# Other slots for the side work of a scan: when four blocks of one core do their parts beside a recurrence

## The chip, the cores and the metric

The kernel runs on one core of a Trainium2 chip. The metric is the device time of one execution in microseconds (us). The median over three runs before the change is 5640.24 us. The engines are named as in the profile: PE (TensorE, matmuls), DVE (VectorE), ACT (ScalarE), POOL (GpSimd) and SP (the queue that issues the DMAs).

## What is computed

A sequence of four blocks on x of 8 batches, 512 steps and 256 columns, each with a residual and a layer norm after it:

```python
x = layernorm(x + L0_attn(x))   # state space scan: z, conv, dt, B, C; state 512 x 128 per batch
x = layernorm(x + L0_ffn(x))    # silu(x w1) * (x w2), then gelu(h1), gelu(h2), w3
x = layernorm(x + L1_attn(x))   # rms norm, q k v, running sums of exp(k) and exp(k)*v, swiglu
x = layernorm(x + L1_ffn(x))    # 8 experts, the best two of each row
# inside L0_attn, step by step:
h = exp(dt * A_mean) * h + dt * B * u ;  y = C . h
y = rms(y) * norm_w * silu(z) ;  out = y @ out_proj
```

The change touches the placing of L0_attn's end (z, the norm of y, its gate, the projection), of the first layer norm, of L0_ffn's gate and up products and of all of L1_attn. The arithmetic of each step stays.

## The kernel before

The program has three phases: `project_phase` (up to 384 us of the span), `stream_phase` (to 4707.6 us, a tail after the last body included) and `expert_phase`. All that is changed lies in `stream_phase`.

The scan there is cut into `CHUNKS` = 8 chunks of 64 steps; the code of a chunk is called a body here, body 0 to body 7. A body has 256 slots. One slot n advances one step t = n // 4 for a pair of batches g = n % 4; two slots are one half step k = n // 2 (128 in a body). Per slot POOL multiplies 384 columns of the state by their decay (`decay_state`, L1548) and DVE adds the outer product that PE has put in a bank (`add`, L1586). Per half step DVE decays the other 128 columns (`keep`, L1576), ACT takes two exponentials for the half step three ahead (`exp_dve`, L1205, from a bank that PE's `e_rows`, L820, fills; `exp_pool`, L1200, whose rows an SP DMA brings), and PE contracts the state with C (`contract`, L832). POOL may run at most four slots ahead of DVE's adds (it waits on `h_ok`), and it needs `exp_pool` of its half step.

Everything else is the mix: the four blocks' work on the chunk before (m = c - 1), and L1_attn of the chunk before that (m - 1). It is put by hand between the steps of the scan. Body 0 has no mix, body 1 has one without L1_attn (`attn` is False), bodies 2 to 7 have all of it. What stands first in each engine's program order runs first:

- PE at slot n: waits for add(n), makes the outer product for slot n + 2, then the mix products whose `_AT` tuple names n, then, at an even n, `e_rows` for half step k + 3; `contract(k)` comes after slot 2k + 1. All mix products share one bank, `M0`; `bank_read` makes each wait until the one before it, in order of slots, has been read.
- ACT at half step k: every 32nd k a copy of y, then `out_of_bank` for slots 2k - 1 and 2k (it copies products out of M0 and takes tanh), then `exp_dve(k + 3)` and `exp_pool(k + 3)`, then `aside(k)`: the norms, squares and roots whose tables name k. A root (L1216 to L1219) loads an activation table, then takes ln and exp.
- DVE at half step k: add(2k), `keep(k + 1)`, mix(2k), add(2k + 1), mix(2k + 1). The mix there holds `silu_z` (L1607), `gate` (L1614, y by rstd by silu z), `add_gated` (L1623) and `statistics` (L1592, L1596), `spread` (L1601, 128 x 4), `silu_gate` (L1628), `hidden` (L1634), `weigh` (L1649), the scans `sum_weights` and `sum_values` (L1657, L1662), `denominator`, `invert`, `divide`.

Chains that cross engines: root_var(1) on ACT, then `spread` on DVE at slot `SPREAD_AT[1]`, then NORM_1, X_SQ, root_x, TO_UNIT on ACT, then the transposes XN on PE, QK, QK_SQ, root_qk, QK_UNIT, the transposes KT and QT, V, and the scans. The other one: Z, silu_z; Y_SQ, root_y; `gate` at `Y_GATE_AT` (the first waits for root_y); GT, O, `add_gated`, root_var(0), NORM_0, XT, then gate and up. Weights come in units of 512 KB into a ring of four slots (`WRING`); their order `FULL` follows `FIRST_USE`, and each is asked for on SP at the half step `DONE_AT` + 3 of the unit four before it.

Of the kernel before, what the change touches and what calls it, by code (L numbers as in the profile page):

```python
# [75 lines left out]
def project_phase(nc, bank, d, used):  # L76
# [3 lines left out]
    with ExitStack() as ctx:  # L80
# [231 lines left out]
        def _(dve):  # L312
# [60 lines left out]
            with dve.Fori(1, BATCH) as s:  # L373
# [52 lines left out]
GATE_AT = (44, 48, 52, 56, 60, 64, 68, 72)
UP_AT = (46, 50, 54, 58, 63, 66, 71, 74)
H1_AT = ((76, 78, 80, 82), (85, 87, 89, 91), (94, 96, 98, 100), (102, 104, 106, 108), (112, 114, 116, 118), (120,
    122, 124, 126), (129, 131, 133, 135), (138, 140, 142, 144))
H2_AT = ((147, 149, 151, 153), (156, 158, 160, 162), (165, 167, 169, 171), (178, 180, 182, 184), (190, 192, 194,  # L430
    196), (204, 206, 208, 210), (214, 216, 218, 220), (224, 226, 228, 230))
SWI_AT = (174, 176, 188, 189)
OUT_AT = (201, 203)
W3_AT = ((234, 235, 236, 237, 238, 239, 240, 241), (242, 243, 244, 245, 246, 247, 248, 249))

USED_AT = {**{("z", i): (n, n) for i, n in enumerate(Z_AT)}, **{("xn", i): (n, n) for i, n in enumerate(XN_AT)},
           **{("qk", i): (n, n) for i, n in enumerate(QK_AT)}, **{("gT", i): (n, n) for i, n in enumerate(GT_AT)},
# [24 lines left out]
TAIL = ("wz", "qk", "wo", "v", "w1a", "w2a", "w1b", "w2b", "swi", "wout", *(f"h1{j}" for j in range(KH)),  # L462
        *(f"h2{j}" for j in range(KH)), "w3a", "w3b")
WRING = 4
SILU_Z_AT = (4, 5, 8, 10)
SILU_GATE_AT = (47, 51, 55, 59, 63, 67, 71, 75)
SILU_SWI_AT = (180, 183)
ROOT_AT = (16, 0, 103)
SPREAD_AT = (35, 3, 210)
ROOT_X_AT = 2  # L470
ROOT_Y_AT = 4
ROOT_QK_AT = 12
Y_GATE_AT = (13, 15, 17, 21)
CW_AT = (80, 87)
CKV_AT = (99, 108)
SEED_AT = 19
KEEP_AT = (54, 68)
DEN_AT = (114, 124)
REC_AT = (121, 131)
DIV_AT = (141, 149)  # L480
STATS_2_AT = (206, 207)
NORM_1_AT = {2: (0, 1, 2, 3)}
X_SQ_AT = {2: (0, 1, 2, 3)}
TO_UNIT_AT = {2: (0,), 3: (1, 2, 3)}
Y_SQ_AT = {0: (0,), 1: (1,), 2: (2, 3)}
QK_SQ_AT = {7: (0,), 8: (1,), 9: (2,), 10: (3,)}
QK_UNIT_AT = {12: ((0, 1), (1, 1)), 13: ((2, 1), (3, 1)), 14: ((0, 0), (1, 0)), 15: ((2, 0), (3, 0))}
NORM_0_AT = {17: (0,), 18: (1, 2, 3)}
NORM_2_AT = {106: (0,), 108: (1, 2, 3)}
LATER = 3  # L490
STORE_AT = (OUT_AT[1] + 16) // 2
# [1832 lines left out]
```

## Time and profile before

| | us |
|---|---|
| median of 3 runs | 5640.24 |
| lowest, highest | 5631.48, 5642.22 |
| profiled execution | 5622.6 |
| its span | 5620.9 |

Slots are located by DVE's adds: each L1586 instruction is one slot, 256 to a body. The first adds of bodies 0 to 7 start at 384.0, 839.4, 1330.2, 1837.2, 2345.9, 2864.7, 3368.3 and 3876.5 us, and the last one at 4379.7. Slot 32 of bodies 1 to 7 starts at 912.0, 1402.6, 1911.1, 2424.1, 2940.0, 3445.2 and 3948.9; slot 80 at 1007.1, 1497.0, 2005.5, 2521.9, 3035.4, 3540.6 and 4043.3. A row of the view by stretch tells for such a window how long each engine was busy; in a stretch where an engine is busy nearly all the time, that engine bounds it.

### The profile page before, as it was taken

What the parts mean: (1) busy time and instruction counts of PE and PEld (TensorE: products, weight loads), DVE (VectorE), ACT (ScalarE), POOL (GpSimd) and SP (SyncE); (2) the same over time, 40 slices, a digit from 0 to 9 for tenths busy, and PEclk for the clock granted to TensorE, in tenths of its full rate; (3) what the DMA queues carried; (4) which work ended last, traced back from release to release, by engine and by line L of the source; (5) the groups of instructions that cost most, each with busy time, mean ns of one, the idle gap of its engine ahead of it and who ended that gap; (6) DMA issues with size and microseconds to landing.
All of it is one profiled execution on the core that took longest, in us unless ns stands there. A gap on an engine that the chain in (4) does not pass through costs nothing. (4 is left out here: it accounts for less than half of the span.)

```text
span 5620.9 us, 68943 instructions
## 1 busy us (share of the span) xinstructions
PE 4751.0 (85%) x20772; PEld 1734.7 (31%) x20772; DVE 3908.9 (70%) x4276; ACT 3396.4 (60%) x3971; POOL 3984.9 (71%) x2256
## 2 busy tenths in 40 slices
PE   5439998998999899998989998998999784399992
PEld 3301112223223222222232232222222343266662
DVE  7848888888988898889889888988998403000003
ACT  4536666778776877777777778777777431111112
POOL 2359998999999899889989998998999100400004
PEclk8755557999999999899999999998999896699996
DMA  2347666777776667766766776776767121233333
GB/s 89 101 155 257 241 240 218 265 255 245 245 259 250 225 250 248 254 227 240 258 235 246 260 262 221 251 266 236 249 248 260 64 75 54 105 107 108 109 111 112
DMA packets 312933, 1138.41 MB, mean 203 GB/s; under 512 B 69664, under 2 KB 123424, under 8 KB 306720
## 3 DMA queue, kind: packets, MB, share of 16 engines
q1 hardware_dynamic: 298688, 1065.24, 53.7%
q0 software_dynamic: 13920, 69.22, 3.6%
q8 instruction: 158, 2.59, 0.2%
q14 instruction: 167, 1.37, 0.1%
HBM read 1077.17 MB, written 69.73 MB: 204 GB/s over the span
## 5 line engine op out<-in xcount | busy, mean ns | idle before, releaser
L1548 POOL TENSOR_TENSOR s_h<-s_decay,s_h 128x768 f32<-128x768 f32 x2048 | 3707.2, 1847 | 288.6 <-ACT s_decay L1200 256.0
L1586 DVE TENSOR_TENSOR s_h<-s_h,bank 128x1024 f32<-128x1024 f32 x2048 | 2470.1, 1215 | 398.3 <-POOL s_h L1548 211.5
L1200 ACT ACTIVATE s_decay<-s_decay,s_a_neg 128x1536 f32<-128x1536 f32 x1024 | 1605.8, 1568 | 117.2 <-DMA s_decay<-dt_rows 116.4
L832 PE MATMUL bank<-s_h,s_cdiag 128*32 128x512 f32 x8192 | 1262.0, 692 | 7.7 <-ACT s_y L1212 6.8
L1205 ACT ACTIVATE bank<-bank,s_a_neg 128x512 f32<-128x512 f32 x1024 | 672.8, 657 | 759.9 <-PE bank L820 757.1
L806 PE MATMUL bank<-s_vrow,s_brow 9*128 9x512 bf16 x4096 | 846.0, 423 | 268.8 <-DVE s_h L1586 241.5
L1576 DVE TENSOR_TENSOR s_h<-bank,s_h 128x512 f32<-128x512 f32 x1024 | 698.8, 682 | 0.6 <-ACT bank L1205 0.5
L806 PEld LDWEIGHTS bank<-s_vrow,s_brow 9*128 9x128 bf16 x4096 | 208.3, 92 | 1498.9 <-issue 1495.5
L944 PE MATMUL bank<-m_mb,m_w 128*128 128x512 f32 x1024 | 521.2, 638 | 0.9 <-ACT m_mb L1278 0.9
L930 PE MATMUL bank<-m_ma,m_w 128*128 128x512 f32 x1024 | 516.3, 633 | 0.0
L820 PE MATMUL bank<-s_drow,s_unit 3*128 3x512 bf16 x1024 | 432.8, 423 | 78.5 <-DMA s_drow<-dt_parts 49.5
L1935 POOL DMA_INDIRECT e_pj<-in_pj,e_rows x23 | 21.6, 939 | 555.0 <-PE bank L1965 554.4
L2066 ACT ACTIVATE e_hid<-bank 128x512 f32<-128x512 f32 x184 | 109.9, 597 | 495.2 <-PE bank L1965 495.2
L1965 PE MATMUL bank<-e_cT,e_fc 128*128 128x512 f32 x736 | 321.8, 595 | 2.0 <-DVE e_cT L2174 2.0
L1965 PE MATMUL bank<-e_pj,e_hid 128*128 128x256 f32 x1472 | 321.4, 379 | 0.0
L2174 DVE COPY e_cT<-bank 128x512 f32<-128x512 f32 x24 | 16.6, 692 | 415.1 <-PE bank L2006 415.1
L832 PEld LDWEIGHTS bank<-s_h,s_cdiag 128*32 128x32 f32 x8192 | 169.8, 114 | 402.5 <-issue 388.4
L1965 PEld LDWEIGHTS bank<-e_pj,e_hid 128*128 128x128 f32 x1472 | 278.0, 190 | 36.9
L820 PEld LDWEIGHTS bank<-s_drow,s_unit 3*128 3x128 bf16 x1024 | 96.4, 94 | 492.1 <-issue 469.0
L944 PEld LDWEIGHTS bank<-m_mb,m_w 128*128 128x128 f32 x1024 | 182.6, 196 | 201.2 <-issue 201.0
L930 PEld LDWEIGHTS bank<-m_ma,m_w 128*128 128x128 f32 x1024 | 181.3, 194 | 200.1 <-issue 200.1
L1925 POOL MEMSET e_eps<- 128x1 f32 x1 | 0.1, 98 | 329.6 <-POOLq L2253 329.6
(197 smaller groups left out, 4098.9 us busy)
## 6 DMA issues: line engine op xcount, KB each, us to landing
s_decay<-dt_rows SPq DMA_DIRECT2D x1024, 768.0 KB, 5.3
m_w<-in_units SPq DMA_DIRECT2D x210, 512.0 KB, 5.1
s_vrow<-v_parts SPq DMA_DIRECT2D x1024, 36.0 KB
s_brow<-b_parts SPq DMA_DIRECT2D x1024, 9.0 KB
v_parts<-p_part SPq DMA_DIRECT2D x24, 512.0 KB, 3.0
slots<-in_x_tiles SPq DMA_DIRECT2D x128, 96.0 KB, 4.7
e_xs<-slots SPq DMA_DIRECT2D x24, 512.0 KB, 9.6
expert_out<-e_made SPq DMA_DIRECT2D x23, 512.0 KB, 9.2
```

What stands on the lines that cost most here:

```text
L806: mm = pe.matmul(bank[:, X0 + n % 2 * PAIR + b], brow[q:q + PAIRS, buf, hf, at * STATE:(at + 1) * STATE], vrow[q:q + PAIRS, buf, hf, at * ...
L820: pe.matmul(bank[:, E0 + hf], unit[q:q + PARTS], drow[q:q + PARTS, buf, t % STEPS], start=True, stop=True).then_inc(e_ps, 1)
L832: mm = pe.matmul(bank[q * 32:(q + 1) * 32, Y0], cdiag[:, hf * LANES + q, at * BLK:(at + 1) * BLK], h[:, t % 2, hf * LANES + q], start=(at ...
L930: mm = pe.matmul(bank[:, j % 4 if tail else M0], w[:, slot, k * P:(k + 1) * P], ma[:, k], start=(k == 0), stop=(k == KH - 1))
L944: mm = pe.matmul(bank[:, j % 4 if tail else M0], w[:, slot, k * P:(k + 1) * P], mb[:, k], start=(k == 0), stop=(k == KH - 1))
L1200: act.activation(decay[:, k % RING], decay[:, k % RING], ACT.Exp, scale=a_neg[:, 1:2]).then_inc(decay_ok, 1)
L1205: act.activation(bank[:, E0 + k % HALVES], bank[:, E0 + k % HALVES], ACT.Exp, scale=a_neg[:, 1:2]).then_inc(e_ok, 1)
L1548: pool.tensor_tensor(h[:, t % 2, g * PAIR:(g + 1) * PAIR, DCOLS:], decay[:, k % RING, g % 2 * PAIR:(g % 2 + 1) * PAIR], h[:, (t + 1) % 2, ...
L1576: dve.tensor_tensor(h[:, t % 2, hf * LANES:(hf + 1) * LANES, 0:DCOLS], bank[:, E0 + hf].rearrange("p (b d) -> p b d", b=LANES), h[:, (t + ...
L1586: dve.tensor_tensor(h[:, t % 2, g * PAIR:(g + 1) * PAIR], h[:, t % 2, g * PAIR:(g + 1) * PAIR], bank[:, X0 + n % 2 * PAIR:X0 + (n % 2 + 1) ...
L1965: mm = pe.matmul(dst, lhs(k), rhs(k), start=(k == 0), stop=(k == n - 1))
L2066: act.activation(hid[:, r, m], bank[:, m % 4], ACT.Gelu).then_inc(up_ok, 1)
```

## The change

Only the tables of slots and half steps change. Of the products, z goes from slots 1, 3, 5, 7 to 0, 2, 4, 6; the transposes of gated y from 21 to 24 to 14, 15, 16, 18; the projection from (27, 28), (30, 31) to (20, 21), (23, 25). L1_attn comes after them: its transposes from 9, 12 to 26, 28, q and k from 14 to 19 to 30 to 36, the transposes of k and q from 32 to 36 to 60, 68 and 64, 70, in between the gate and up products, which begin at 41 for 44, and v from 39, 42 to 73, 74. The norms and squares of half steps 2 and 3 are spread over 4 to 12; root_var(1) goes from half step 0 to 3 and its spread from slot 3 to 7; the gate of y goes from slots 13 to 21 to 10 to 14 while root_y stays at half step 4; root_qk goes from 12 to 21 and the q and k norms from 12 to 15 to 23 to 29. From slot 79 on, scans, reciprocals and a few more move by one to six slots. With the slots the order of the weight units changes: wz, wo, qk, w1a, w2a, w1b, w2b, v for wz, qk, wo, v, w1a, w2a, w1b, w2b.

```diff
--- before.py
+++ after.py
@@ -414,22 +414,22 @@
 X_CREDIT = BUFS * GROUPS * STEPS
 E_CREDIT = BUFS * HALVES * STEPS
 
-Z_AT = (1, 3, 5, 7)
-XN_AT = (9, 12)
-QK_AT = (14, 15, 17, 19)
-GT_AT = (21, 22, 23, 24)
-O_AT = ((27, 28), (30, 31))
-KT_AT = (32, 34)
-QT_AT = (35, 36)
-XT_AT = (40, 43)
-V_AT = (39, 42)
-GATE_AT = (44, 48, 52, 56, 60, 64, 68, 72)
-UP_AT = (46, 50, 54, 58, 63, 66, 71, 74)
-H1_AT = ((76, 78, 80, 82), (85, 87, 89, 91), (94, 96, 98, 100), (102, 104, 106, 108), (112, 114, 116, 118), (120,
+Z_AT = (0, 2, 4, 6)
+XN_AT = (26, 28)
+QK_AT = (30, 31, 34, 36)
+GT_AT = (14, 15, 16, 18)
+O_AT = ((20, 21), (23, 25))
+KT_AT = (60, 68)
+QT_AT = (64, 70)
+XT_AT = (37, 40)
+V_AT = (73, 74)
+GATE_AT = (41, 45, 49, 54, 57, 61, 65, 69)
+UP_AT = (43, 48, 51, 55, 59, 63, 67, 72)
+H1_AT = ((75, 77, 79, 81), (86, 88, 90, 92), (94, 96, 98, 100), (102, 104, 106, 108), (112, 114, 116, 118), (120,
     122, 124, 126), (129, 131, 133, 135), (138, 140, 142, 144))
 H2_AT = ((147, 149, 151, 153), (156, 158, 160, 162), (165, 167, 169, 171), (178, 180, 182, 184), (190, 192, 194,
     196), (204, 206, 208, 210), (214, 216, 218, 220), (224, 226, 228, 230))
-SWI_AT = (174, 176, 188, 189)
+SWI_AT = (174, 176, 187, 188)
 OUT_AT = (201, 203)
 W3_AT = ((234, 235, 236, 237, 238, 239, 240, 241), (242, 243, 244, 245, 246, 247, 248, 249))
 
@@ -462,30 +462,30 @@
 TAIL = ("wz", "qk", "wo", "v", "w1a", "w2a", "w1b", "w2b", "swi", "wout", *(f"h1{j}" for j in range(KH)),
         *(f"h2{j}" for j in range(KH)), "w3a", "w3b")
 WRING = 4
-SILU_Z_AT = (4, 5, 8, 10)
-SILU_GATE_AT = (47, 51, 55, 59, 63, 67, 71, 75)
-SILU_SWI_AT = (180, 183)
-ROOT_AT = (16, 0, 103)
-SPREAD_AT = (35, 3, 210)
-ROOT_X_AT = 2
+SILU_Z_AT = (3, 5, 8, 9)
+SILU_GATE_AT = (44, 48, 52, 56, 60, 64, 68, 72)
+SILU_SWI_AT = (179, 181)
+ROOT_AT = (14, 3, 103)
+SPREAD_AT = (33, 7, 210)
+ROOT_X_AT = 9
 ROOT_Y_AT = 4
-ROOT_QK_AT = 12
-Y_GATE_AT = (13, 15, 17, 21)
-CW_AT = (80, 87)
-CKV_AT = (99, 108)
-SEED_AT = 19
-KEEP_AT = (54, 68)
-DEN_AT = (114, 124)
-REC_AT = (121, 131)
-DIV_AT = (141, 149)
-STATS_2_AT = (206, 207)
-NORM_1_AT = {2: (0, 1, 2, 3)}
-X_SQ_AT = {2: (0, 1, 2, 3)}
-TO_UNIT_AT = {2: (0,), 3: (1, 2, 3)}
-Y_SQ_AT = {0: (0,), 1: (1,), 2: (2, 3)}
-QK_SQ_AT = {7: (0,), 8: (1,), 9: (2,), 10: (3,)}
-QK_UNIT_AT = {12: ((0, 1), (1, 1)), 13: ((2, 1), (3, 1)), 14: ((0, 0), (1, 0)), 15: ((2, 0), (3, 0))}
-NORM_0_AT = {17: (0,), 18: (1, 2, 3)}
+ROOT_QK_AT = 21
+Y_GATE_AT = (10, 11, 13, 14)
+CW_AT = (79, 91)
+CKV_AT = (96, 102)
+SEED_AT = 36
+KEEP_AT = (57, 68)
+DEN_AT = (117, 125)
+REC_AT = (122, 131)
+DIV_AT = (145, 151)
+STATS_2_AT = (205, 206)
+NORM_1_AT = {4: (0,), 5: (1,), 6: (2, 3)}
+X_SQ_AT = {6: (0, 1), 7: (2,), 9: (3,)}
+TO_UNIT_AT = {10: (0,), 11: (1, 2), 12: (3,)}
+Y_SQ_AT = {0: (0,), 2: (1,), 3: (2, 3)}
+QK_SQ_AT = {15: (0,), 16: (1,), 17: (2,), 19: (3,)}
+QK_UNIT_AT = {23: ((0, 1),), 24: ((1, 1), (2, 1)), 25: ((3, 1),), 27: ((0, 0), (1, 0)), 29: ((2, 0), (3, 0))}
+NORM_0_AT = {15: (0,), 16: (1, 2), 17: (3,)}
 NORM_2_AT = {106: (0,), 108: (1, 2, 3)}
 LATER = 3
 STORE_AT = (OUT_AT[1] + 16) // 2
```

## Rows read from the trace of the kernel before

**Rows 1.** by stretch: its bounds, length, busy us (instructions), clock, DMA.

```profile
384.00:839.40 455.40, 436.44 (x1656) 59.75 (x1656) 384.53 (x384) 279.09 (x274) 455.40 (x258) 0.50 0.69 245
839.40:912.00 72.60, 60.80 (x263) 17.48 (x261) 60.15 (x61) 45.65 (x58) 63.23 (x34) 0.71 0.57 211
1330.20:1402.60 72.40, 59.24 (x289) 19.09 (x286) 58.29 (x63) 67.06 (x113) 59.66 (x33) 0.89 0.63 218
1837.20:1911.00 73.80, 60.07 (x288) 19.53 (x285) 57.35 (x62) 67.21 (x113) 58.72 (x33) 0.86 0.58 212
1911.00:2005.50 94.50, 84.37 (x422) 26.26 (x422) 87.86 (x97) 70.24 (x87) 85.36 (x48) 1.00 0.68 236
3876.50:3948.90 72.40, 59.24 (x288) 19.08 (x285) 58.16 (x62) 67.06 (x113) 59.62 (x33) 0.89 0.62 223
```

**Rows 2.** POOL in body 0, in body 3's slots 0-31, 32-79.

```profile
L1548 POOL TENSOR_TENSOR s_h<-s_decay,s_h 128x768 f32<-128x768 f32 x258 | 459.0, 1812 | 0.0
...
L1548 POOL TENSOR_TENSOR s_h<-s_decay,s_h 128x768 f32<-128x768 f32 x33 | 60.5, 1864 | 15.1 <-ACT s_decay L1200 14.9
...
L1548 POOL TENSOR_TENSOR s_h<-s_decay,s_h 128x768 f32<-128x768 f32 x48 | 86.7, 1841 | 9.1 <-ACT s_decay L1200 9.1
```

**Rows 3.** groups of DVE in body 3, slots 0 to 31.

```profile
L1607 DVE SCALAR_TENSOR_TENSOR m_mb<-m_ma,m_mb 128x512 f32<-128x512 f32 x4 | 3.4, 857 | 8.3 <-ACT m_ma L1249 8.3
L1614 DVE SCALAR_TENSOR_TENSOR s_y<-s_y,m_sm,m_mb 128x512 f32<-128x512 f32 x4 | 5.5, 1371 | 0.0
L1601 DVE SCALAR_TENSOR_TENSOR m_shift<-m_mv,m_rstd 128x4 f32<-128x4 f32 x1 | 1.0, 977 | 1.4 <-ACT m_rstd L1219 1.4
L1623 DVE TENSOR_TENSOR m_xa<-m_xa,bank 128x512 f32<-128x512 f32 x1 | 0.7, 689 | 2.9 <-PE bank L882 2.9
L1592 DVE BATCH_NORM_STATS2 m_st<-m_xa 128x6 f32<-128x256 f32 x2 | 0.7, 414 | 0.0
```

**Rows 4.** ACT in order of time, body 3: start, length, instruction.

```profile
1842.59 1.28 ACT L1216 ACT_TABLE_LOAD   x1
1853.19 2.07 ACT L1240 ACTIVATE m_x<-m_x,m_shift,m_rstd 128x256 f32<-128x256 f32 x4
...
1862.26 0.63 ACT L1249 ACTIVATE m_ma<-m_mb 128x512 f32<-128x512 f32 x1
1862.79 0.64 ACT L1205 ACTIVATE bank<-bank,s_a_neg 128x512 f32<-128x512 f32 x1
```

**Rows 5.** PE in order of time, the products of z in body 3.

```profile
1840.88 3.49 PE L863 MATMUL bank<-m_w,m_cT 128*128 128x512 f32 x4
1845.83 1.98 PE L863 MATMUL bank<-m_w,m_cT 128*128 128x512 f32 x4
...
1861.00 3.67 PE L863 MATMUL bank<-m_w,m_cT 128*128 128x512 f32 x4 [5.62 <-ACT m_mb L1245]
```

**Rows 6.** DVE in slots 32-79; a line's least, median, most ns.

```profile
L1628 DVE SCALAR_TENSOR_TENSOR m_mb<-m_ma,m_mb 128x512 f32<-128x512 f32 x8 | 10.5, 1314 | 1.0 <-ACT m_ma L1273 1.0
L1634 DVE SCALAR_TENSOR_TENSOR m_ma<-bank,m_half_s,m_mb 128x512 f32<-128x512 f32 x8 | 6.0, 746 | 2.2 <-PE bank L916 2.1
...
L1601 DVE SCALAR_TENSOR_TENSOR m_shift<-m_mv,m_rstd x24: 161/620/4048, 920.3 to 4700.9; 128x4 f32<-128x4 f32 x24
```

**Rows 7.** groups of ACT in body 3, slots 0 to 31.

```profile
L1200 ACT ACTIVATE s_decay<-s_decay,s_a_neg 128x1536 f32<-128x1536 f32 x16 | 25.1, 1567 | 0.0
L1205 ACT ACTIVATE bank<-bank,s_a_neg 128x512 f32<-128x512 f32 x16 | 10.4, 652 | 2.7 <-PE bank L820 2.7
L1309 ACT ACTIVATE m_u<-m_qk 128x256 f32<-128x256 f32 x8 | 3.2, 407 | 0.0
L1304 ACT ACTIVATE m_qk<-bank 128x512 f32<-128x512 f32 x4 | 2.3, 587 | 2.8 <-PE bank L982 2.8
L1314 ACT ACTIVATE m_qk<-m_qk,m_sm 128x256 f32<-128x256 f32 x6 | 2.7, 499 | 0.0
```

**Rows 8.** DVE in order of time, body 3: the start of add(3).

```profile
1841.84 1.21 DVE L1586 TENSOR_TENSOR s_h<-s_h,bank 128x1024 f32<-128x1024 f32 x1
```

## The prediction, made before the change was run

> **What bounds the kernel now.** Read the stretches first [rows 1]. Body 0 has no mix: 455.4 us for 256 slots, POOL busy in all of them, so 1.779 us a slot is the floor that POOL sets, and 32 slots cost 56.9 us, 48 slots 85.4 us. The other bodies take more. In bodies 2 to 7 slots 0 to 31 take 72.4, 73.8, 78.2, 75.3, 76.9 and 72.4 us (the first two and the last stand in [rows 1]; all follow from the slot times given with the profile above), 74.8 on the mean, 17.9 above the floor. Slots 32 to 79 take 95.3 on the mean (body 3: 94.5), 9.9 above it. So 28 us a body are lost in the part that the change rearranges, 6 x 28 = 168 us in the six: no placing can give back more there.
>
> Next, who is late. POOL's groups [rows 2] show 15.1 us idle in body 3's first 32 slots, 14.9 of it until ACT's exponential of the decay (L1200), and 9.1 us in the next 48. DVE's view of the same 32 slots [rows 3] shows what is behind it: DVE waits 8.3 us for the tanh of z (L1607 waiting on L1249), 1.4 for the root before `spread`, 2.9 for the projection. ACT in order of time [rows 4] shows the cause of the 8.3: four norms from 1853.19 on, then squares, a root, the square of y, and only at 1862.26 the tanh, with the next exponential at 1862.79. PE stands still 5.62 us meanwhile, since the bank isn't read, and is back at the lower clock afterwards: the four matmuls of one z take 3.67 us at 1861.00 against 1.98 at 1845.83 [rows 5].
>
> In slots 32 to 79 no engine has such a gap: DVE is busy 87.86 of 94.5 us [rows 1]. That stretch is bound by DVE, with the pairs of `silu_gate` (1.314 us, [rows 6]) and `hidden` (0.746) every four slots.
>
> **The change part by part.** *Spreading norms, squares, roots.* ACT has 67.21 us busy in 73.8 in body 3's first 32 slots [rows 1]. Out of them go both table loads before tanh (z is at half steps 0 to 3 now, with no root between): 2 x 1.28 [rows 4]; the load of root_qk, 1.28; the six norms of q and k that the window holds, 6 x 0.50 = 3.0; and three of four tiles of q and k, each a copy and two squares, 3 x (0.59 + 2 x 0.41) = 4.2 [rows 7]. Into them come root_var(0), at least its load of 1.28, and one norm, 0.5. Net 11.0 - 1.8 = 9.2 off: ACT wants 58 us, about POOL's floor of 56.9, and no longer more. One load (before the last z's tanh) is gone for good, since each of the roots keeps its own and the gate's tanh now needs two: 1.28 a body, hidden beside POOL where ACT isn't late. The Trainium skill (ScalarE: Activation LUTs, What ACT_TABLE_LOAD costs) puts a switch at 1283 ns of load and about 1380 ns of drain, 2.66 us. The load is 1.28 here, but the tanh starts right behind it, so the drain isn't seen; by the page ACT would get 1.4 us more a body, under 9 us in six.
>
> *What the burst costs the path.* Gone are the 8.3 us in which DVE waits for tanh, and the 1.4 before `spread` in slot 3 [rows 3]: 9.7 us a body.
>
> *What takes their place.* Two things, both worked out from body 3. First, z(0) now stands in slot 0, ahead of `e_rows` and of the outer product for slot 3. PE is at the lower clock there (3.49 us for one z, [rows 5]); the product begins some 1.1 us sooner than the 1840.88 of now, ends near 1843.3, and the outer product that add(3) needs comes behind it, near 1844.1, where add(3) now starts at 1841.84 [rows 8]. That is 2.3 us. Second, root_var(1) comes after `exp_pool(6)` of half step 3, and its `spread` stands only one slot behind, in slot 7 (now half step 0 and slot 3: three slots apart). From the start of z(3) to the end of the root: z 1.98, copy about 0.6, tanh 0.63, exponentials 0.64 and 1.57, the load 1.28, ln and exp at least 0.4: 7.1 us [rows 4, 5, 7]. DVE has add(7) to do in that time, 1.2, and about 0.4 pass in PE's outer product ahead of z(3): 5.5 us idle. It may be 4, if ACT is ahead there, or 7.5, if ACT is already late by the 2 us of z(0). I take 5.5. The wait of `gate` for root_y (slot 10 behind half step 4, now slot 13) is 0 to 1.5 us; by then DVE has been held in slot 7, so I take nothing. `add_gated` waits 2.9 us for the projection [rows 3]; the projection has the same form at slots 20, 21, 23, 25, so it stays. Sum for slots 0 to 31: -9.7 + 2.3 + 5.5 = -1.9 us a body: 72.9 in place of 74.8.
>
> A row says the same from another side. Body 1 has no L1_attn, none of its norms, squares and roots, and ACT is busy 45.65 us only; yet its slots 0 to 31 take 72.60 us [rows 1], 2.2 less than the mean of the others. An ACT freed by 20 us has brought little by itself. (PE's clock is 0.71 there against 0.86, so it is a bound from one side and no proof.)
>
> *Slots 32 to 79.* DVE loses the second `add_gated` and its statistics to the first stretch, 0.69 + 2 x 0.41 = 1.5 us [rows 3], where POOL's floor leaves room for them. What remains is the same number of `silu_gate` and `hidden` in the same rhythm. The transposes of k and q now stand between up and gate (slots 60, 64, 68, 70): each waits on PE for DVE's `hidden` of its own slot, some 0.7 + 1.3 + 0.75 us behind the add, and holds `e_rows` and, behind it, both exponentials. The decay that needs them is six slots off, so it is covered as long as ACT isn't late; without this cover it is up to 2 us at each of four places. I take 0, as DVE is the bound there. `weigh` stays in the stretch, `sum_weights` at slot 79 was at 80. So -1.5.
>
> *The rest.* The eight weight units of 512 KB: the tightest wait is w1b, asked for at half step 15 and used at 28; none comes near. SP's order changes by nothing else. From slot 79 on the scans, reciprocal and divisions move by 1 to 6 slots. DVE instructions with both inputs in SBUF take very different times beside POOL: `spread`, 4 columns wide, has 0.16, 0.62 and 4.05 us as least, median and most [rows 6]. I take 0 for the shift of all of these, and 4 us either way for a body as their bounds.
>
> Sum: 6 x (-1.9 - 1.5) = -20 us; body 1 keeps its time (z(0) costs it the same and its gates come earlier), the tail is the same program. The profiled execution took 5622.6 us (5620.9 of span), 17.6 under the median; from it 5602, and beside the median of 5640.2: **5620 us**. By itself this case has a range of 5595 to 5640.
>
> **The rivals.** *The burst was the whole loss.* If the two waits that I put in its place are covered by POOL's four slots of lead, only the engines' work counts: 58 us for ACT, 57.35 + 1.5 + about 1 for DVE. Slots 0 to 31 then take about 61 us, 13.8 less, and with the 1.5 us it is 6 x 15.3 = 92: 5548 us. For it: nothing else in the first 32 slots is busy over 61 us. Against: body 1. Chance 0.18.
>
> *Slower: DVE blocks at `spread` in slot 7 and again behind it.* POOL(12) needs add(8), so while DVE waits POOL runs dry as well, and PE, which needs the add, falls to the lower clock as at 1861.00 [rows 5]. Then slots 8 to 14 bring two silu_z and four gates to DVE, 0.86 and 1.37 us each [rows 3], 7.2 us in seven slots, and the first transposed y waits for the last gate in its own slot (14). If the wait is 7.5, the gate for root_y 1.5, and the even slots of the transposes in 60 to 70 cost half of their bound (4), a body pays 2 + 1.5 + 4 = 7.5 more than forecast, 4.1 more than now: +25 us, 5665. It decides once ACT reaches the root more than 9 us after add(6) ends. Chance 0.27.
>
> *Slower: scans in a worse phase.* The Trainium skill (SBUF — State Buffer, Who interferes with whom) says that GpSimd and a DVE instruction with two SBUF inputs lock each other out for a whole instruction. The rows on `spread` look like it. As a mechanism of this kernel: one moved instruction in each of six bodies meets two of POOL's instead of none, 4.05 - 0.16 = 3.9 us [rows 6], +23 us against the forecast: 5643, no difference from now; two of them: 5666. Chances 0.05 and 0.03.
>
> *No difference.* The second attention's products, spread between gates, take back what the first stretch gains: 5640. Chance 0.10.
>
> **How the numbers follow.** Forecast 0.37, whole loss 0.18, slower by `spread` 0.27, phase 0.05 and 0.03, no difference 0.10. 0.2% is 11 us, about what a measurement of this kernel can tell from no change. Of the forecast's own range 0.06 lies within it. Faster: 0.31 + 0.18 = 0.49. Same: 0.06 + 0.05 + 0.10 = 0.21. Slower: 0.27 + 0.03 = 0.30. The range reaches into the first two rivals: 5550 to 5675.
>
> **What would show it.** Right: in bodies 2 to 7 the 8.3 us at L1607 are gone, DVE waits about 5 us before L1601 in slot 7, add(3) waits for PE about 2 us, slots 0 to 31 take about 73 us, slots 32 to 79 about 94. Wrong towards faster: slots 0 to 31 at 61 to 66. Wrong towards slower: L1601 waits over 7 us, or POOL's idle time behind L1200 in slots 60 to 79 grows over 2 us a body, or the scans after slot 79 show 6 us where they had 2.

## The result: 1.4% slower

| | before | after |
|---|---|---|
| median, us | 5640.86 (4 runs) | 5717.95 (4 runs) |
| lowest, highest | 5631.48, 5642.22 | 5708.54, 5728.23 |
| profiled execution | 5622.6 | 5728.23 |
| its span | 5620.9 | 5726.5 |

The ratio is 1.0142, 95% interval 1.0123 to 1.0161: about 80 us slower by it (77 between the medians), where 20 faster was forecast and the range ended at 5675. The page of the changed kernel, its groups of instructions (busy us, mean ns, idle time before and who ended it):

```profile
L1548 POOL TENSOR_TENSOR s_h<-s_decay,s_h 128x768 f32<-128x768 f32 x2048 | 3710.8, 1850 | 374.9 <-ACT s_decay L1200 290.6
L1586 DVE TENSOR_TENSOR s_h<-s_h,bank 128x1024 f32<-128x1024 f32 x2048 | 2474.1, 1217 | 506.3 <-PE bank L806 260.6
...
L806 PE MATMUL bank<-s_vrow,s_brow 9*128 9x512 bf16 x4096 | 852.3, 429 | 324.8 <-DVE s_h L1586 296.3
```

DVE waits before its adds 506.3 us, just over half of it for PE's outer products (260.6); in the kernel before it was 398.3 us, of which 181.0 for PE. That is the first sign: the engines have not got more to do, the adds come late.

By stretch, as in [rows 1]: bodies 1 and 3 of the changed kernel, slots 0 to 31 and 32 to 79, and behind them the one stretch of before (body 1, slots 32 to 79) that isn't shown above. Columns: bounds, length, busy of PE, PEld, DVE, ACT, POOL, clock, DMA share, GB/s.

```profile
839.40:912.60 73.20, 60.39 (x274) 19.00 (x272) 61.12 (x66) 47.47 (x61) 63.14 (x34) 0.73 0.59 210
912.60:1015.00 102.40, 92.27 (x396) 23.99 (x393) 82.44 (x90) 67.38 (x78) 85.99 (x49) 0.84 0.63 223
1865.60:1942.70 77.10, 62.24 (x281) 20.47 (x282) 61.40 (x68) 56.31 (x83) 60.80 (x34) 0.74 0.58 215
1942.70:2047.80 105.10, 95.84 (x438) 28.25 (x436) 86.08 (x93) 82.68 (x119) 89.41 (x50) 0.97 0.64 231
```

```profile
912.00:1007.10 95.10, 86.38 (x399) 24.23 (x398) 86.68 (x95) 67.42 (x79) 84.24 (x47) 0.89 0.64 223
```

The means over bodies 2 to 7, from the starts of the adds:

| slots | before | after | body 1 before | body 1 after |
|---|---|---|---|---|
| 0 to 31 | 74.8 | 77.1 | 72.6 | 73.2 |
| 32 to 79 | 95.3 | 105.2 | 95.1 | 102.4 |
| 80 to 255 | 338.4 | 339.2 | 323.1 | 324.9 |

A body costs 13.1 us more, body 1 9.7: 88 us up to the last add. The profiled executions differ by 106; the other 17 lie behind the last add, where the program is the same (1241 us in the one of before, 1250 to 1272 in all other profiles of this study). They are not the change's.

Three quarters of the loss are in slots 32 to 79, where the prediction had -1.5. Of the 9.9 us there, 2.4 are one `sum_weights` that the change moved from slot 80 to slot 79, so over the edge of the stretch; the other 7.5 are new, and slots 80 to 255, without it, are 3.2 us slower and not 0.8. The loss is there in body 1 too, which has no second attention and no `sum_weights`: 7.3 us. ACT did get lighter in slots 0 to 31, 56.31 us for 67.21 [rows 1], as forecast (58). It moved to slots 32 to 79: 82.68 for 70.24.

DVE in body 3, slots 0 to 31 (answers to [rows 3]):

```profile
L1586 DVE TENSOR_TENSOR s_h<-s_h,bank 128x1024 f32<-128x1024 f32 x33 | 39.8, 1212 | 5.8 <-PE bank L806 5.3 <-POOL s_h L1548 0.4
...
L1614 DVE SCALAR_TENSOR_TENSOR s_y<-s_y,m_sm,m_mb 128x512 f32<-128x512 f32 x4 | 6.3, 1584 | 0.2 <-ACT m_sm L1219 0.2
L1607 DVE SCALAR_TENSOR_TENSOR m_mb<-m_ma,m_mb 128x512 f32<-128x512 f32 x4 | 5.8, 1455 | 0.0
...
L1623 DVE TENSOR_TENSOR m_xa<-m_xa,bank 128x512 f32<-128x512 f32 x2 | 1.4, 688 | 3.6 <-PE bank L882 3.6
...
L1601 DVE SCALAR_TENSOR_TENSOR m_shift<-m_mv,m_rstd 128x4 f32<-128x4 f32 x1 | 0.2, 164 | 5.9 <-ACT m_rstd L1219 5.9
```

The wait for tanh (L1607) is gone, the one before `spread` (L1601) is there with 5.9 us, and the four `silu_z` take 5.8 us in place of 3.4 [rows 3].

DVE in slots 32 to 79 of body 3, first the changed kernel (answers to [rows 6]), then the adds of the kernel before:

```profile
L1586 DVE TENSOR_TENSOR s_h<-s_h,bank 128x1024 f32<-128x1024 f32 x49 | 58.6, 1214 | 13.3 <-PE bank L806 13.3
...
L1628 DVE SCALAR_TENSOR_TENSOR m_mb<-m_ma,m_mb 128x512 f32<-128x512 f32 x8 | 6.9, 866 | 2.3 <-ACT m_ma L1273 2.3
L1634 DVE SCALAR_TENSOR_TENSOR m_ma<-bank,m_half_s,m_mb 128x512 f32<-128x512 f32 x8 | 6.0, 751 | 1.6 <-PE bank L916 1.4
...
L1649 DVE TENSOR_TENSOR m_u<-m_u,bank 128x512 f32<-128x512 f32 x2 | 1.4, 688 | 1.8 <-PE bank L1009 1.8
```

```profile
L1586 DVE TENSOR_TENSOR s_h<-s_h,bank 128x1024 f32<-128x1024 f32 x49 | 58.3, 1210 | 0.2 <-POOL s_h L1548 0.2
```

0.2 us of waiting before adds have become 13.3, all for PE. DVE didn't get more work there (86.08 us busy for 87.86); it no longer bounds the stretch. The eight `silu_gate` take 6.9 us now, 10.5 before [rows 6], for the same work: part of the new waiting is made up by shorter instructions, so the waits are not yet the price.

The rhythm shows where the adds wait. PE in body 5 of the changed kernel, from the gate product of slot 57 to the up product of slot 59 (start, length, instruction), and DVE's add of slot 60:

```profile
3043.44 0.39 PE L806 MATMUL bank<-s_vrow,s_brow 9*128 9x512 bf16 x2 [0.61 <-DVE s_h L1586]
3043.76 1.98 PE L906 MATMUL bank<-m_cT,m_w 128*128 128x512 f32 x4
3045.67 1.06 PE L832 MATMUL bank<-s_h,s_cdiag 128*32 128x512 f32 x8
3046.67 0.40 PE L806 MATMUL bank<-s_vrow,s_brow 9*128 9x512 bf16 x4
3046.90 0.38 PE L820 MATMUL bank<-s_drow,s_unit 3*128 3x512 bf16 x1
3047.20 1.98 PE L916 MATMUL bank<-m_cT,m_w 128*128 128x512 f32 x4
...
3047.20 1.22 DVE L1586 TENSOR_TENSOR s_h<-s_h,bank 128x1024 f32<-128x1024 f32 x1 [1.05 <-PE bank L806]
```

The same gate product in the kernel before, at an even slot (60):

```profile
2999.56 1.98 PE L906 MATMUL bank<-m_cT,m_w 128*128 128x512 f32 x4
3001.48 0.39 PE L820 MATMUL bank<-s_drow,s_unit 3*128 3x512 bf16 x1
3001.48 0.39 PE L806 MATMUL bank<-s_vrow,s_brow 9*128 9x512 bf16 x2
3001.80 1.07 PE L832 MATMUL bank<-s_h,s_cdiag 128*32 128x512 f32 x8
3002.80 0.39 PE L806 MATMUL bank<-s_vrow,s_brow 9*128 9x512 bf16 x2
```

At an odd slot the product (1.98 us) and `contract` (1.06) stand together between two outer products. The outer products of the next two slots then come together, late (x4 at 3046.67, two matmuls each), and the add waits 1.05. At an even slot an outer product stands between the two (3001.48). The change has 13 of its 16 gate and up products at odd slots, the kernel before has two.

### The profile page after: what moved, and what is told of

Its sections match the earlier page's. It is cut to its first block and busy times, and to the rows that moved or that the text cites. A ratio compares the mean times of both kernels' runs of the same rounds, so it can differ in the third digit from the quotient of the medians.

```text
span 5726.5 us, 68937 instructions
## 1 busy us (share of the span) xinstructions
PE 4808.6 (84%) x20772; PEld 1745.0 (30%) x20772; DVE 3889.9 (68%) x4276; ACT 3394.8 (59%) x3965; POOL 3989.0 (70%) x2256
## 5 line engine op out<-in xcount | busy, mean ns | idle before, releaser
L1586 DVE TENSOR_TENSOR s_h<-s_h,bank 128x1024 f32<-128x1024 f32 x2048 | 2474.1, 1217 | 506.3 <-PE bank L806 260.6
L832 PE MATMUL bank<-s_h,s_cdiag 128*32 128x512 f32 x8192 | 1279.7, 701 | 5.0 <-ACT s_y L1212 5.0
```

The lines of the kernel that those rows point to most:

```text
L832: mm = pe.matmul(bank[q * 32:(q + 1) * 32, Y0], cdiag[:, hf * LANES + q, at * BLK:(at + 1) * BLK], h[:, t % 2, hf * LANES + q], start=(at ...
L1586: dve.tensor_tensor(h[:, t % 2, g * PAIR:(g + 1) * PAIR], h[:, t % 2, g * PAIR:(g + 1) * PAIR], bank[:, X0 + n % 2 * PAIR:X0 + (n % 2 + 1) ...
```

## The experiments

Ratios are against the kernel before on the same chip, and versions are compared through them. "Alone" means put into the kernel before.

### What the root's new place costs, and the tables behind slot 79

The changed kernel with root_var(1) back at half step 0; spread stays in slot 7:

```diff
-ROOT_AT = (14, 3, 103)
+ROOT_AT = (14, 0, 103)
```

> The changed kernel with root_var(1) back at half step 0, its spread left in slot 7. Theory A (the wait of 6.2 us before the spread is lost time, and PE falls to the lower clock behind it): slots 0 to 31 of bodies 2 to 7 fall from 77.1 to 69 to 72 us, the kernel by 30 to 45 us to 5673 to 5688. Theory B (DVE would have waited for something else there, the products of z at even slots or the tanh behind the table load): below 2 us a body, 5706 to 5718.

5697.17 us, ratio 1.0102 (1.0074 to 1.0129) for 1.0142 of the change: about 23 us come back, though the two intervals overlap a little. In the profile the wait at L1601 is 0, DVE waits 2.5 us a body for tanh and 2.8 for root_y (L1614) instead, and slots 0 to 31 take 71.6 us on the mean for 77.1, 3.2 less than before. So by its own stretch the first part of the change is a gain once the root isn't right ahead of its reader. What the wait does besides stopping DVE, in the changed kernel, ACT, DVE and PE of body 3:

```profile
1886.42 1.28 ACT L1216 ACT_TABLE_LOAD   x1
1887.71 0.30 ACT L1217 ACTIVATE m_rstd<-m_mv,m_const 128x4 f32<-128x4 f32 x1
...
1888.28 0.16 DVE L1601 SCALAR_TENSOR_TENSOR m_shift<-m_mv,m_rstd 128x4 f32<-128x4 f32 x1 [5.94 <-ACT m_rstd L1219]
...
1889.76 0.61 PE L806 MATMUL bank<-s_vrow,s_brow 9*128 9x512 bf16 x2 [5.37 <-DVE s_h L1586]
...
1893.86 1.08 PE L832 MATMUL bank<-s_h,s_cdiag 128*32 128x512 f32 x4
```

PE stands still 5.37 us as well and comes back at the lower clock (granted 0.50, which is 1.2 GHz, in the 4 us behind): its outer product takes 0.61 us for 0.39, four contraction products 1.08 where eight took 1.06. The granted clock of slots 0 to 31 is 0.74 in body 3; body 3 of before had 0.86 [rows 1]. In body 4 it is 0.74 too, 0.81 with the root at half step 0, and was 0.81 before.

Only the tables from slot 79 on (scans, reciprocals, divisions, swiglu), alone:

> The kernel before with only what the change moves from slot 79 on: scans, denominators, reciprocals, divisions, swiglu, statistics, the second h1. By the traces slots 80 to 255 are 0.8 us a body slower after the change though one scan of 2.4 us has left them for slot 79: 3 us a body or +15 to +20 us. If the long scans of 6.4 and 7.0 us that three bodies show before are only a matter of phase, it is within 10 us of before.

5635.43 us over 10 runs, ratio 0.9999 (0.9987 to 1.0011): no cost that these runs can tell, 7 us being the width of the interval to either side.

The norms, squares and roots spread over half steps 2 to 5, alone:

```diff
-ROOT_X_AT = 2
-ROOT_Y_AT = 4
+ROOT_X_AT = 3
+ROOT_Y_AT = 5
...
-NORM_1_AT = {2: (0, 1, 2, 3)}
+NORM_1_AT = {2: (0, 1), 3: (2, 3)}
...
```

(The lines left out move the squares of x, y, q and k, the scaling of x, and the transposes and q and k products behind them by up to three slots.)

> The kernel before with only its burst of half steps 2 and 3 thinned out: norms and squares two and two, root_x at 3, the unit scaling at 4 and 5, the transposes behind it at 12, 13, q and k at even slots 14 to 20, root_y at 5; root_var(1) and its spread stay. Theory (spreading is good, what is around it in the change is bad): DVE's waits of 5.2 us a body for the tanh of z fall to 1 to 3, slots 0 to 31 from 74.8 to 71 to 73, the kernel -10 to -20 us, 5615 to 5625. Rival (ACT's load is the same, so POOL waits as long, elsewhere): within 8 us of before.

5677.29 us, ratio 1.0081 (1.0064 to 1.0098), slower where a gain was expected. The wait for tanh only fell from 5.2 to 4.5 us a body, and `gate` (L1614) waits 3.7 us for root_y, which is now in half step 5; slots 0 to 31 take 79.4 us for 74.8. Spreading a burst moves the last of its results, and here that one has a reader close by. That this wait is the whole of the 4.6 us was not tested.

The earlier z, put into the kernel before together with the late ups of the next section (these by themselves: ratio 0.9991):

```diff
-Z_AT = (1, 3, 5, 7)
+Z_AT = (0, 2, 4, 6)
-SILU_Z_AT = (4, 5, 8, 10)
+SILU_Z_AT = (3, 5, 8, 10)
```

> The kernel before with the ups at 47, 51, ..., 71, 74 (that alone: 0.1% under before, slots 0 to 31 at 73.9 us) and z at slots 0, 2, 4, 6, silu_z at 3, 5, 8, 10. If the wait for tanh of z behind the burst of norms is a loss that an earlier z takes away (4.0 us a body in that run): slots 0 to 31 take 71 to 72 us, the time is 10 to 25 us under before. If z in slot 0 and the burst only move the wait to the add of slot 3 and to the gate: 73 to 75 us, within 10 us of before.

5655.31 us, ratio 1.0037 (1.0019 to 1.0055), which is neither of the two outcomes that had been written down. The wait for tanh is gone, but slots 0 to 31 take 80.6 us in bodies 2 to 7, 73.9 with the late ups only; in body 1, which has no burst, 67.8 for 71.5. In body 3 the wait sits at `keep`, for ACT's exponential behind the same burst, with 8.9 us before adds for PE:

```profile
L1586 DVE TENSOR_TENSOR s_h<-s_h,bank 128x1024 f32<-128x1024 f32 x32 | 38.7, 1214 | 11.3 <-PE bank L806 8.9 <-POOL s_h L1548 2.3
L1576 DVE TENSOR_TENSOR s_h<-bank,s_h 128x512 f32<-128x512 f32 x16 | 10.9, 683 | 6.3 <-ACT bank L1205 6.3
...
L1607 DVE SCALAR_TENSOR_TENSOR m_mb<-m_ma,m_mb 128x512 f32<-128x512 f32 x4 | 4.3, 1085 | 0.0
```

### Which slots gate and up take

Gates and ups at odd slots, alone:

```diff
-GATE_AT = (44, 48, 52, 56, 60, 64, 68, 72)
-UP_AT = (46, 50, 54, 58, 63, 66, 71, 74)
-SILU_GATE_AT = (47, 51, 55, 59, 63, 67, 71, 75)
+GATE_AT = (43, 47, 51, 55, 59, 63, 67, 71)
+UP_AT = (45, 49, 53, 57, 62, 65, 70, 73)
+SILU_GATE_AT = (46, 50, 54, 58, 62, 66, 70, 74)
```

(v and the transposes of x also one slot earlier, to make room.)

> The kernel before with the gate and up products, their silus, v and the transposes of the normed x one slot earlier, nothing else: gate and up now stand in 14 odd slots where they stood in 2. Theory 1 (parity): at an odd slot a product of 1.75 us and the contraction of 1.0 us stand together between two outer products of PE, so that DVE waits about 1.05 us before the next even add, as the trace after shows at slot 60. Then DVE's idle time before its adds in slots 32 to 79 grows from 0.8 to some 10 to 12 us a body and the kernel takes +60 to +85 us, 5700 to 5725. Theory 2 (the second attention between the gates is what costs): nothing of it moves here, so the kernel stays within 10 us of before.

5683.24 us, ratio 1.0082 (1.0056 to 1.0108). DVE's waits before adds in slots 32 to 79 go from 0.8 to 10.4 us a body, those for silu_gate and hidden go down in turn, and the stretch takes 100.0 us for 95.3. So the odd slots alone cost 46 us (32 to 61 by the interval) where the change costs 80, with the moved v and x transposes in it.

The other way round, the changed kernel with all gates and ups at even slots (42, 46, ... and 44, 48, ...):

> The changed kernel with gate at 42, 46, ... 70, up at 44, 48, ... 72, silu_gate three slots behind its gate, the transposes of k and q at 61, 69 and 65, 71: still between the gates. Theory 1 (parity): slots 32 to 79 lose 8 to 12 us a body, the kernel comes down from 5718 to 5640 to 5665. Theory 2 (second attention between the gates): only the gate whose silu stood two slots behind it gains, 2 to 4 us a body, 5690 to 5705.

5712.12 us, ratio 1.0127 (1.0101 to 1.0154): 8 us back, not measurable, where 50 or more were expected. But body 1, slots 32 to 79, takes 96.2 us for 102.4 and 95.1 before:

```profile
910.70:1006.90 96.20, 85.69 (x396) 23.13 (x393) 86.67 (x90) 66.46 (x77) 85.65 (x49) 0.89 0.67 240
```

In that body only gates, ups and their silus differ from the changed kernel, so their slots make 6.2 of its 7.3 us. Bodies 2 to 7 take 105.9: slot 73 alone has 6.3 us, where `hidden` waits 3.4 for an up product that stands behind the transposes of q at slot 71. That pointed to the second attention.

Two smaller edits of the changed kernel. Gate 3 at slot 53 for 54, since silu_gate follows it after two slots only and slot 56 takes 6.2 us:

> The changed kernel with the fourth gate product at slot 53 in place of 54, so that its silu at 56 is three slots behind it, as for the others, and not two. Both theories: the waits of 2.3 and 0.8 us in slot 56 go, the outer product after it comes late by 1 us instead (53 is odd): slots 56 to 63 fall from 19.5 to 16 or 17 us a body, -15 to -25 us, 5693 to 5703. If it doesn't fall, the slot waits for something else.

5727.59 us, ratio 1.0155 (1.0128 to 1.0182), where 5693 to 5703 was expected: slots 56 to 63 do gain 2.5 us, but slots 32 to 55 lose 3.9, of it 2.2 in slot 55, some in slots that the edit didn't touch. And the contraction issued behind the next even slot's outer product:

```diff
 if n % 2 == 0:
+    for late in owed:
+        contract(*late)
+    owed.clear()
...
-        contract(c, k)
+        owed.append((c, k))
```

> The changed kernel, its slots untouched, with each contraction issued not at the end of its half step but behind the outer product of the next even slot. Parity theory: an odd slot's product has now only itself between two outer products, so DVE's waits of about 1.05 us before even adds go: its idle time before adds in slots 32 to 79 falls from 13.5 to under 6 us a body, the gate stretch by 3 to 7 us a body, the kernel to 5670 to 5700; the products of z at even slots now share with a contraction and may give some of it back. If instead the products themselves or ACT are what DVE waits for, nothing changes: 5710 to 5725.

5732.64 us, ratio 1.0168 (1.0150 to 1.0186), where 5670 to 5700 was expected. Body 3, slots 32 to 79 (by the inserted lines the adds are L1592, `silu_gate` L1634):

```profile
L1592 DVE TENSOR_TENSOR s_h<-s_h,bank 128x1024 f32<-128x1024 f32 x47 | 56.1, 1215 | 8.0 <-PE bank L806 7.8
...
L1634 DVE SCALAR_TENSOR_TENSOR m_mb<-m_ma,m_mb 128x512 f32<-128x512 f32 x8 | 13.1, 1642 | 5.6 <-ACT m_ma L1279 5.6
```

PE's order does what the theory says: adds wait 6.2 us a body for 13.5 in the changed kernel. But the stretch gains 1.9 us only, since the eight `silu_gate` take 13.2 us for 7.3 and wait 1.4 longer for ACT. A wait before an add is so not worth its length, and what the product and `contract` side by side cost is not shown by the 13.3 us of waiting. Slots 80 to 255 lose 3.6 us (body 1: 7.4), perhaps because most products there stand at even slots and now have the contraction beside them; this was not looked at further.

The odd rhythm taken apart. Only the ups later, each in the slot of its silu_gate (alone):

```diff
-UP_AT = (46, 50, 54, 58, 63, 66, 71, 74)
+UP_AT = (47, 51, 55, 59, 63, 67, 71, 74)
```

> The kernel before with each up product one slot later, at an odd slot (47, 51, 55, 59, 63, 67, 71, 74; before has two of them there), the gates stay even. If any product at an odd slot costs about 1 us, as the run with gates and ups at odd slots seemed to say: five more of them, 1 us each, seven bodies, +20 to +35 us. Rival from the slot times of before: the five slots from 60 to 64, with up at 63, take 9.25 us, those from 56 to 60, with up at 58, 9.73, so the up beside its own silu_gate saves 0.5 us each time, -12 to -20 us; then only the gate product is bad at an odd slot.

5633.73 us over 12 runs, ratio 0.9991 (0.9974 to 1.0007): no difference that these runs can tell, though slots 32 to 79 take 92.4 us for 95.3. So an up product at an odd slot, beside its own silu_gate, does no harm. The same rhythm one slot earlier, so that the gates are odd:

> The kernel before with the rhythm of the run with late ups (gate, three slots on its silu_gate and the up product together), but all of it one slot earlier: gates at odd slots (43, 47, ..., 71), silu_gate and ups at even ones (46, 50, ..., 74); v and the transposes of x one slot earlier to make room, as in the run with gates and ups at odd slots. The one with gates at even slots took 92.4 us for slots 32 to 79 and was 0.1% under before. Theory (a gate product beside the contraction, between two outer products, delays the next add): slots 32 to 79 take 97 to 100 us, DVE waits 5 to 10 us a body before its adds there, the time is +20 to +40 us against before. Rival (what cost in that run was the up product one slot ahead of silu_gate, not the gate's slot): 92 to 94 us, adds wait under 2 us, -10 to +5 us.

5659.09 us, ratio 1.0034 (1.0020 to 1.0049). Body 1, slots 32 to 79, late ups and then the same one slot earlier:

```profile
913.20:1004.90 91.70, 87.51 (x398) 24.37 (x398) 85.33 (x95) 66.98 (x79) 85.46 (x47) 0.89 0.67 227
```

```profile
913.20:1010.20 97.00, 86.83 (x398) 24.57 (x398) 83.37 (x96) 68.39 (x79) 85.17 (x47) 0.89 0.66 226
```

5.3 us for the same work; adds wait 10.3 us where they waited 3.8. In bodies 2 to 7 it is 97.7 for 92.4, but 3.0 of these 5.3 lie in slots 32 to 39, where the moved v and x transposes are. So gates at odd slots cost 2 to 5 us a body.

### Where the second attention stands

k, q and v between the gates, with h1's first products squeezed to make room (alone):

> The kernel before with only the second attention's last products put among gate and up, these left at their even slots: transposes of k at 59, 61, of q at 65, 67, v at 73, 76, the seed at half step 36, the first slots of h1 at 78, 79. Theory that the odd gates cost and the second attention doesn't: under 2 us a body, within 12 us of before. Rival, as the stretch of slots 64 to 79 with even gates suggests (40.4 us there against 30.6): each transposition makes the next up or gate wait for ACT or DVE, 4 to 8 us a body, +25 to +50 us.

5698.63 us, ratio 1.0124 (1.0103 to 1.0145). Body 1 lost 6.1 us too, so h1 had a part. Without it, k at 59 and 61, q at 65 and 67, v at 69 and 73:

> The kernel before with the transposes of k and q between gate and up (59, 61 and 65, 67), v at 69 and 73; h1 and all else stay. The run that did this together with a squeezed start of h1 took +64 us, but its body 1, which has no second attention, lost 6.1 us too. If the attention between the gates is the cause: +35 to +55 us, all in slots 56 to 80, with hidden and weigh waiting some 5 and 3 us. If h1's squeezed start was: 0 to +15 us, body 1 unchanged.

5701.29 us, ratio 1.0101 (1.0072 to 1.0130), body 1 unchanged (490.9). `hidden` waits 7.3 us in body 4's slots 32 to 79, `weigh` 4.5. Then k and q at the even slots which late ups leave free (58, 62, 66, 70), and the same idea in the changed kernel:

> The kernel before with the ups at 47, 51, ..., 71, 74 (that alone was 0.1% under before, slots 32 to 79 at 92.4 us) and with the second attention's k and q between gate and up, but at the even slots that this leaves free (58, 62 and 66, 70); v at 69 and 73 as in the run that had k and q at 59, 61, 65, 67 and was 58 us slower. Theory (ACT reads the product of an odd slot behind both exponentials of the half step before, that of an even slot ahead of them, and PE's next product and hidden wait for it): slots 32 to 79 take 93 to 96 us, hidden and weigh wait under 3 us together, the time is -10 to +15 us against before. Rival (k, q and v cost wherever they stand between gates): slots 32 to 79 take 100 us or more, +35 to +60 us.

> The changed kernel with root_var(1) back at half step 0 (that alone gave back 21 us) and gates at 42, 46, ..., 70, silu_gate and ups at 45, 49, ..., 73, k at 60 and 64, q at 68 and 72, v at 67 and 71: whatever ACT reads stands at an even slot. Theory (the slot's parity for ACT's products and the near spread are the whole loss; y first gains 3.2 us a body): slots 0 to 31 take 71.6 us, slots 32 to 79 take 93 to 98 (the sum_weights of 2.4 that was moved in among them), the time is 5600 to 5645. Rival (the attention between the gates costs wherever it stands): slots 32 to 79 stay above 102, the time at 5680 to 5700.

5690.35 us, ratio 1.0087 (1.0068 to 1.0105), and 5694.05 us, ratio 1.0095 (1.0077 to 1.0113). Both times are the rival's; my theory of the slot's parity fell for k and q. Their traces show another order. The first of the two in body 4, slots 58 to 61, PE, ACT and DVE:

```profile
2491.59 0.63 ACT L1273 ACTIVATE m_ma<-m_mb 128x512 f32<-128x512 f32 x1
2492.12 0.64 ACT L1205 ACTIVATE bank<-bank,s_a_neg 128x512 f32<-128x512 f32 x1
2492.40 0.66 PE L990 MATMUL bank<-m_ident,m_qk 128*128 128x128 f32 x4
...
2492.70 1.56 ACT L1200 ACTIVATE s_decay<-s_decay,s_a_neg 128x1536 f32<-128x1536 f32 x1
2494.16 0.60 ACT L1319 ACTIVATE m_u<-bank 128x512 f32<-128x512 f32 x1
...
2494.82 3.33 PE L916 MATMUL bank<-m_cT,m_w 128*128 128x512 f32 x4 [1.44 <-ACT m_u L1319]
...
2498.26 0.75 DVE L1634 SCALAR_TENSOR_TENSOR m_ma<-bank,m_half_s,m_mb 128x512 f32<-128x512 f32 x1 [2.72 <-PE bank L916]
```

Gate, k and up go through the one bank M0 in turn (v stands between a gate and its up too, at 69 and 73). k's transposes end at 2493.06, but ACT has by then gone into its two exponentials (2.2 us) and takes k out at 2494.16; up starts behind that, at the lower clock (3.33 us for 1.98), and `hidden` holds DVE. ACT's copy of the gate, ahead of these exponentials, had itself waited 2.1 us for the product, and waits 4.9 for the next one, which stands behind the late `hidden`: three products pass through the bank more slowly than four slots go by.

In the changed kernel both k and the first q stand between up and the next gate, and `hidden` waits 1.6 us in all (above). The second q, at slot 70, does stand between gate (69) and up (72), and `hidden` behind it waits nothing; with q at 71 and gate at 70 it waited 3.4. So the order alone doesn't decide, the slots left between the three count as well. By this the bank is not the change's own loss. The test of the order is the changed kernel with the root at half step 0, gates at 42, 46, ..., 70, silu_gate and ups together at 45, 49, ..., 73, and k and q directly ahead of a gate:

```diff
-KT_AT = (60, 64)
-QT_AT = (68, 72)
-V_AT = (67, 71)
+KT_AT = (58, 62)
+QT_AT = (66, 70)
+V_AT = (74, 75)
```

(against the last run; the norms of q and k up to two half steps earlier, h1's first four at 77 to 83)

> As the changed kernel with root_var(1) at half step 0, gates at 42, 46, ..., 70 and silu_gate and ups at 45, 49, ..., 73, but k and q each directly ahead of a gate, in its slot (58, 62 and 66, 70): the order in the bank is up, hidden, k, gate. v at 74 and 75, h1's first four at 77 to 83, the norms of q and k one to two half steps earlier. Theory (k and q cost only where they stand between a gate and its up, since up then waits for ACT's exponentials): hidden waits under 2 us a body in slots 56 to 80 (7.9 in the run before), slots 32 to 79 take 95 to 99 us, the time is 5620 to 5655. Rival (they cost between the gates in any order): slots 32 to 79 above 103, 5680 or more.

5658.15 us over 12 runs, ratio 1.0044 (1.0025 to 1.0062): 0.5% under the last run, 0.98% or 55 us under the changed kernel. `hidden` in slots 32 to 79 of body 4, the last run and this one:

```profile
L1634 DVE SCALAR_TENSOR_TENSOR m_ma<-bank,m_half_s,m_mb 128x512 f32<-128x512 f32 x8 | 5.9, 743 | 8.4 <-PE bank L916 8.4
```

```profile
L1586 DVE TENSOR_TENSOR s_h<-s_h,bank 128x1024 f32<-128x1024 f32 x50 | 59.7, 1213 | 14.4 <-PE bank L806 10.0 <-POOL s_h L1548 4.4
...
L1634 DVE SCALAR_TENSOR_TENSOR m_ma<-bank,m_half_s,m_mb 128x512 f32<-128x512 f32 x8 | 6.0, 745 | 0.2
```

That looks like the order theory (8.4 us down to 0.2), but the last run was no clean case of it. Its waits are 5.6 us in slot 62 and 2.5 in slot 66, both behind k, and none behind q. The first begins with k's transposes, which wait for the last norm of q and k on ACT and leave PE at the lower clock (the up behind them takes 3.78 us for 1.98):

```profile
2486.12 1.09 PE L990 MATMUL bank<-m_ident,m_qk 128*128 128x128 f32 x4 [2.73 <-ACT m_qk L1314]
```

The new version has these norms earlier (that wait is 0.8 us) and v out of the gates, so only the 2.5 us speak for the order by themselves; the 29 us between the two runs are not split further. The order's clean case is the trace of slots 58 to 61 above, where the norms had long been done. The time is 3 us over the band that the theory gave, since slots 32 to 79 take 102.7 us and not 95 to 99: adds wait 13.1 us a body there, 10.0 of the 14.4 in body 4 for PE.

Last, the whole attention ahead of the gates, as before, behind y (the changed kernel with q, k and v packed into slots 29 to 43, gates, ups and h1's first products where they were before, root at half step 0):

> The changed kernel with y's part still first, but root_var(1) back at half step 0, the gate and up products and h1's first four back at their slots of before, and all of the second attention's k, q and v packed ahead of the gates. Theory (the loss is the near spread, the odd gates and the attention between the gates; y first is harmless and even gains 3.2 us a body, as measured with the root at 0): slots 0 to 31 take 71.6 us, slots 32 to 79 take 95 to 98, and the time is 5615 to 5630, under the 5634 of before. Rival (something else of the change costs: the order y first, the tables behind slot 79): it stays above 5670.

5753.64 us, ratio 1.0214 (1.0186 to 1.0242): the rival's side, and the slowest of all. Body 1, without the attention, takes 69.2 us for slots 0 to 31 and 95.2 for 32 to 79, as good as before or better; bodies 2 to 7 take 114.5 for 32 to 79. PE in body 4:

```profile
2476.96 1.09 PE L891 MATMUL bank<-m_ident,m_xa 128*128 128x128 f32 x4 [9.12 <-ACT m_xa L1240]
```

PE stands 9.12 us before the transposes of x, because ACT has squares of q and k, a root, four norms and two rounds of exponentials ahead of x's last norm. With y first and the attention whole behind it the burst on ACT is back, and larger.

## Why the prediction was wrong, point by point

- **Slots 32 to 79 are bound by DVE, the rhythm is the same: -1.5.** This step failed; measured +9.9. "The same rhythm" was nearly true of the distances, but I costed only DVE's side, where the row of before showed 87.86 busy of 94.5. PE's order within a slot was not looked at: a gate at an odd slot brings product and contraction between two outer products, and DVE, the bound before, now waits 13.5 us a body for its adds. `sum_weights`, named as moved to slot 79, was put at nothing and brings 2.4 us into the stretch. The regular group of four slots takes 8.4 us (slots 60 to 63) for 8.0 (56 to 59 of before); the rest are single slots such as 56 (6.2 us) and `sum_weights`. That the slots of gates and ups are the cause is shown by body 1 (+7.3 us, +1.1 with all of them at even slots) and by the runs with odd gates (46 us for gates and ups, 19 with the gates alone). How much of it is PE's order and how much the single slots is not settled: with the order changed the waits halved and the time stayed.
- **The transposes between the gates take 0 to 2 us at four places.** For the changed kernel near the truth: bodies 2 to 7 lose 9.9 us where body 1, without them, loses 7.3, and 2.4 of the difference is sum_weights. The reading of the tables was off in one place: slot 70 is between gate and up, not between up and gate, and only there does the transpose not wait for `hidden`. That the place matters at all I had not seen; with k, q and v between gate and up the kernel before takes 49 to 57 us more.
- **Gone: 8.3 + 1.4 us.** The waits went away as said, but 8.3 is body 3's. In bodies 2 to 7 of before the wait for tanh is 6.3, 8.3, 2.3, 4.7, 3.3 and 6.4 us, 5.2 on the mean (and the one before `spread` 1.9). A term read from one body was multiplied by six: 7.1 us go, not 9.7.
- **In their place: 5.5 before spread, 2.3 before add(3).** Measured 5.94 and 2.2 in body 3 (add(3) starts 6.8 us behind add(0), it was 4.6; 0.9 to 2.2 in the six bodies). Right, mechanism and size, of the two waits. But the second is no loss of the whole stretch: all waits before its adds are 5.7 us a body, and were 6.2. With `add_gated` waiting 3.9 us for 2.9, DVE's waits come out about even, and the loss is in its busy time, 61.1 us for 59.0. Not priced were 1.5 us of add_gated and its statistics that I took out of the second stretch and did not add to the first, the longer `silu_z`, and PE at the lower clock after the wait (0.74 for 0.86). Sum for slots 0 to 31: forecast -1.9, measured +2.3.
- **The rest: 0.** Right for the tables behind slot 79 as far as the runs tell (ratio 0.9999). Slots 80 to 255 take 0.8 us more all the same, with sum_weights' 2.4 gone from them; why is open.
- **The rivals.** "Slower: DVE blocks at spread" named a true cause (23 us of the 80) and the sign, at 5665; its condition, the root reached over 9 us behind add(6), was not met (5.8 us in five bodies, 7.3 in body 2), so that its sign came out is in part luck. It was not the main loss. Body 1 had been used for what it says of ACT, and then left at no change; it has the gates and ups too, and lost 9.7 us.

What stays open: the causes don't add up (root 23, odd gates 19 to 46, against 80), the intervals of the single steps are 10 to 30 us wide, and the best version rebuilt from the changed kernel, with 55 us given back, is still 25 us behind before. No version here beats the kernel before by more than its interval.

## What to carry to other kernels

Before a product is moved by one slot, write down PE's queue for both slots: what stands between two steps of the critical recurrence decides which engine waits, and a busy share of another engine doesn't show it. The length of that wait isn't yet the price; only the stretch's own length is. Products that share one bank form a chain with their readers: before one is put between a pair whose second half an engine waits for, count the slots that are left for all three. And a wait that is to be saved is read in all bodies, not in the one at hand.

## What was not expected of the hardware

A table load is 1.28 us and the activation behind it starts at once (1886.42 and 1887.71 above), while the one ahead of it had ended 0.02 us before: no drain is seen on either side. The Trainium skill (ScalarE: Activation LUTs, What ACT_TABLE_LOAD costs) has 1283 ns for the load, as here, and about 1380 ns of drain, which no run here shows. The four `silu_z` of one body took 2.9 to 4.9 us in bodies 2 to 7 of the kernel before and 5.8 in body 3 of the changed one, for the same work. Short ones stand on the whole in bodies in which DVE waited long among them (2.9 us with 6.3 and 6.4 of waiting, 3.4 with 8.3, 4.9 with 2.3), long ones where it didn't wait (5.8 with 0, and 6.6 in body 1 of before). A wait taken away is so in part paid back in longer instructions: with the wait of 5.2 us gone, DVE's busy time in slots 0 to 31 rose by 2.2 us, 1.5 of it moved work. It is clearest in the run with the late contraction, where 7.3 us less of waiting came with 5.9 us more in eight `silu_gate`. The adds, which read a bank, stay at 1.21 us in every body. The Trainium skill (SBUF — State Buffer, Who interferes with whom) says that GpSimd and a DVE instruction with two SBUF inputs lock each other out; these times go the way it says, and no run here tests it.
